# A decoder layer's set-up code: weight halves loaded first, projections side by side, two down-weight loads moved up

## The reference, cut to what matters

```python
def reference(x, ctx, Wi, Wf, Wg, w_norm, Wo, w, u, w_gate_up, w_down):
    # 1: i, f, g = x @ Wi.T, x @ Wf.T, x @ Wg.T; a = sigmoid(f)
    #    h = linear_scan(a, silu(i) * (1 - a)); xg = h * silu(g)
    #    y = xg * rsqrt(mean(xg**2) + eps) * w_norm;  x = layernorm(x + y @ Wo.T)
    # 2: x = layernorm(x + wkv(w, u, k=x, v=ctx))     # running sums of exp(k)*v and exp(k)
    # 3: gate, up = quant(x) @ quant(w_gate_up).T;  h = silu(gate) * up
    #    x = layernorm(x + quant(h) @ quant(w_down).T)
    return x
```

## Time and profile before

| | us |
|---|---|
| median of 3 runs | 411.18 (409.6 to 411.26) |
| profiled execution | 412.55 |
| its span | 410.1 |
| TensorE busy | 370.8 (90%) |
| VectorE busy | 353.6 (86%) |
| ScalarE busy | 318.7 (78%) |
| GpSimd busy | 219.3 (53%) |

### The profile page before, as it was taken

One profiled execution on the slowest core, in us unless ns is written; L12 is line 12 of the kernel. 1 busy time (PEld: TensorE's weight loads), 2 busy tenths in 40 slices (PEclk: granted clock), 3 DMA queues, 4 the chain that ended last, 5 costly groups with the idle time before them and its releaser, 6 DMA issues.

```text
span 410.1 us, 7960 instructions
## 1 busy us (share of the span) xinstructions
PE 370.8 (90%) x2774; PEld 289.9 (71%) x2774; DVE 353.6 (86%) x639; ACT 318.7 (78%) x420; POOL 219.3 (53%) x281
## 2 busy tenths in 40 slices
PE   7699899889997899999999999999999999659992
PEld 7698799768964788669775977497749785335541
DVE  3879898888788988988899988998899889898895
ACT  3677599769848989599959996799769994974782
POOL 1546772753355725674377535673566356644561
PEclk9989999999999999999999999999999999959999
DMA  7977456011110013000500050004000300000002
GB/s 257 361 273 269 164 195 243 2 53 27 59 46 0 2 48 134 0 28 2 179 2 27 2 179 2 26 0 154 25 0 26 129 0 0 26 2 18 36 26 77
DMA packets 12842, 31.74 MB, mean 77 GB/s; under 512 B 2038, under 2 KB 5132, under 8 KB 12812
## 3 DMA queue, kind: packets, MB, share of 16 engines
q1 hardware_dynamic: 12812, 31.35, 21.9%
HBM read 27.14 MB, written 4.21 MB: 76 GB/s over the span
## 4 chain that ended last, share of the span: by engine, by line
ACT 25%; PE 24%; issue 15%; DVE 14%; POOL 10%; POOLq 0%; ACTq 0%; DVEq 0%
PE proj_ps L530 13%; PE slot_ps L639 8%; POOL ring L1352 4%; ACT L1056 3%; ACT hqT L1021 2%; ACT ring L1014 2%; ACT L1060 2%; DVE inp L1545 2%; DVE x_max L1670 2%; ACT gate L897 2%; POOL gate L1292 2%; ACT q_state L962 2%; ACT q_state L956 2%; ACT gate L935 1%; ACT xqT L998 1%
## 5 line engine op out<-in xcount | busy, mean ns | idle before, releaser
L639 PE MATMUL slot_ps<-w1q,xqT 128*128 128x512 bf16 (+1 forms) x384 | 83.1, 367 | 5.1 <-DVE ring L1702 2.9
L1352 POOL TENSOR_TENSOR ring<-ring 128x512 f32<-128x512 f32 (+1 forms) x48 | 59.6, 1248 | 42.3 <-ACT ring L1007 41.1
L639 PEld LDWEIGHTS slot_ps<-w1q,xqT 128*128 128x128 bf16 x384 | 36.0, 99 | 44.7 <-issue 4.4
L530 PE MATMUL proj_ps<-x_high,proj_high 128*128 128x256 f32 x384 | 65.3, 292 | 1.7 <-DVE inp L1567 1.0
L530 PE MATMUL proj_ps<-x_high,proj_low 128*128 128x256 f32 x384 | 62.2, 284 | 0.0
L530 PE MATMUL proj_ps<-x_low,proj_high 128*128 128x256 f32 x384 | 62.0, 283 | 0.0
L530 PEld LDWEIGHTS proj_ps<-x_high,proj_high 128*128 128x128 f32 x384 | 53.6, 190 | 3.8 <-issue 1.6
L530 PEld LDWEIGHTS proj_ps<-x_high,proj_low 128*128 128x128 f32 x384 | 53.5, 191 | 0.0
L530 PEld LDWEIGHTS proj_ps<-x_low,proj_high 128*128 128x128 f32 x384 | 53.0, 189 | 0.0
L1327 POOL TENSOR_TENSOR den<-den,q_state 128x512 f32<-128x512 f32 x16 | 21.2, 1328 | 49.3 <-ACT q_state L962 48.9
L1007 ACT ACTIVATE ring<-ring,zero_bias,x_scale 128x512 f32<-128x512 f32 (+1 forms) x48 | 37.0, 775 | 9.5 <-DVE ring L1699 9.4
(11 more groups left out here) (157 smaller groups left out, 835.5 us busy)
## 6 DMA issues: line engine op xcount, KB each, us to landing
ring<-w_gate_up_dram SPq DMA_DIRECT2D x11, 512.0 KB, 4.2
forget<-xT_dram SPq DMA_DIRECT2D x8, 512.0 KB, 3.4
x_sb<-x_dram SPq DMA_DIRECT2D x8, 512.0 KB, 3.8
c_sb<-cT_dram SPq DMA_DIRECT2D x8, 512.0 KB, 4.5
out_dram<-late SPq DMA_DIRECT2D x12, 256.0 KB, 2.1
late<-w_down_dram SPq DMA_DIRECT2D x2, 704.0 KB, 6.9
ring<-w_down_dram SPq DMA_DIRECT2D x2, 704.0 KB, 4.2
scale_rows<-scratch_dram SPq DMA_DIRECT2D x2, 704.0 KB, 6.0
```

The costliest lines, as they stand in the source:

```text
L530: last = nc.tensor.matmul(out, a, b, start=(i == 0), stop=(i == len(terms) - 1))
L639: last = nc.tensor.matmul(slot_ps[:, s, half * 512:half * 512 + width], xqT[:, par, d, t * P:(t + 1) * P], w1q[:, d, half * I + at:half * ...
L1352: nc.gpsimd.tensor_tensor(hid, hid, gate_buf[:, at:at + width], ALU.mult).then_inc(hid_ready, 1)
```

## The change

It changes the order of the start-up part on all five queues, and nothing in the iteration or in the tail.

- SyncE: half (0,1) comes ahead of load 0, both i halves ahead of the column vectors and load 1; both output halves follow the g halves. Loads 8 and 9 are now the first two down rows (table `LOAD_AT`, from the place q in the queue to the load meant), and the pairs 8, 9, 10 follow as loads 10, 11, 12. Loads 13 and 14 remain down rows. The context `load_c(0)`, `store_scales` and `load_xT(2)` change places.
- TensorE: projections (0,0) and (0,1), (0,2) and (0,3), (1,0) and (1,1), (1,2) and (1,3) stand next to each other. Of the fillers, 28 in front of the first output projection, 16 in front of projection (1,0) and 36 in front of output projection (1,0) are gone. The key turning of batch 0 follows projection (1,1).
- VectorE, ScalarE, GpSimd: `weigh_rows`, `keep_rows` and `round_rows` move to match; `mean_square(0)` stands behind load 6 instead of 7; `layer_norm_2(0)` and the rest of the second norm move; the chunks' `scale_products`, `silu` and `hidden` of batch 0 are interleaved with WKV of batch 1 differently.

```diff
@@ -50,9 +50,10 @@
 RING = 3
 ROWS = 2 * IB + DB
-HOMES = [q % RING for q in range(UP_LOADS)] + [RING, RING + 1, 2, 1]
-
-SPREADS = [(0, IB, 6), (IB, 2 * IB, UP_LOADS), (2 * IB, ROWS, LOADS)]
+LOAD_AT = [0, 1, 2, 3, 4, 5, 6, 7, UP_LOADS, UP_LOADS + 1, 8, 9, 10, UP_LOADS + 2, UP_LOADS + 3]
+HOMES = [0, 1, 2, 0, 1, 2, 0, 1, RING, RING + 1, 2, 0, 1, 2, 1]
+
+SPREADS = [(0, IB, 6), (IB, 2 * IB, LOADS - 2), (2 * IB, ROWS, LOADS)]
 PROJ = 6
 U_CAP, U_FREE = 72.0, 16.0
...
@@ -462,39 +466,39 @@
             load_half((0, 0))
             load_xT(0)
+            load_half((0, 1))
             load_rows(0)
-            load_half((0, 1))
+            load_half((1, 0))
+            load_half((1, 1))
             load_columns()
-            load_half((1, 0))
             load_rows(1)
-            load_half((1, 1))
+            load_half((2, 0))
             load_rows(2)
-            load_half((2, 0))
             load_half((2, 1))
+            load_half((OUT_PROJ, 0))
+            load_half((OUT_PROJ, 1))
             load_rows(3)
             load_x(0)
             load_rows(4)
-            load_half((OUT_PROJ, 0))
             load_rows(5)
-            load_half((OUT_PROJ, 1))
-            load_rows(11)
+            load_rows(8)
             load_xT(1)
             load_rows(6)
             load_rows(7)
-            store_scales(0)
-            load_rows(8)
-            load_c(0)
-            load_rows(12)
             load_rows(9)
             load_rows(10)
-            load_rows(13)
+            load_c(0)
+            load_rows(11)
+            store_scales(0)
+            load_rows(12)
             spread_scales(0)
             load_x(1)
+            load_xT(2)
+            load_rows(13)
             store_scales(1)
             load_rows(14)
             load_c(1)
             spread_scales(1)
-            load_xT(2)
             load_x(2)
             store_scales(2)
             spread_scales(2)
...
@@ -687,13 +691,13 @@
                 pe.wait_ge(rows_rounded, q + 1)
                 wait(pe, rows_kept, q - 1)
-                if q == UP_LOADS:
-                    pe.wait_ge(scales_read, 2)
+                if LOAD_AT[q] >= UP_LOADS and row_slot(q) == 1:
+                    pe.wait_ge(scales_read, 1 if q < LOADS - 2 else 2)
                 if q == LOADS - 1:
                     pe.wait_ge(rows_kept, q)
                     pe.wait_ge(mlp_read, 2)
                 r = row_home(q)
-                if q < UP_LOADS:
+                if LOAD_AT[q] < UP_LOADS:
                     o = slot_16(row_slot(q), 2 * D).rearrange("p (d a o) -> p d a o", d=DB, a=2)
                     for a in range(2):
                         for d in range(DB):
...
@@ -710,6 +714,8 @@
             def turn_scales(k):
                 first, end, loads = SPREADS[k]
                 pe.wait_ge(row_scale_ready, loads)
+                if k == 1:
+                    pe.wait_ge(rows_kept, LOAD_AT.index(UP_LOADS + 1) + 1)
                 nc.tensor.transpose(scales_ps(k), row_scale[:, first:end],
                                     identity[:, :]).then_inc(scales_turned, 1)
...
@@ -760,61 +766,58 @@
             warm_up()
             warm_up()
             project(0, 0)
+            project(0, 1)
             turn_rows(0)
-            project(0, 1)
+            project(0, 2)
+            project(0, 3)
             turn_rows(1)
-            project(0, 2)
+            project(0, 4)
             turn_rows(2)
-            project(0, 3)
-            project(0, 4)
             project(0, 5)
-            for q in range(3, 6):
-                turn_rows(q)
-            turn_scales(0)
-            keep_busy(28)
-            pe.wait_ge(xg_ready, 1)
+            turn_rows(3)
             keep_busy(28)
             project_out(0, 0)
             sum_squares(0)
             project_out(0, 1)
-            turn_rows(6)
-            turn_rows(7)
-            keep_busy(16)
+            turn_rows(4)
+            turn_rows(5)
             project(1, 0)
-            turn_rows(8)
+            project(1, 1)
+            turn_scales(0)
             turn_keys(0, 0)
             turn_keys(0, 1)
-            project(1, 1)
-            turn_scales(1)
+            turn_rows(6)
             project(1, 2)
-            turn_rows(9)
             project(1, 3)
-            turn_rows(10)
+            turn_rows(7)
             project(1, 4)
             project(1, 5)
             keep_busy(28)
             turn_values(0, 0)
             turn_values(0, 1)
-            turn_rows(11)
-            keep_busy(36)
+            turn_rows(8)
+            turn_rows(9)
             project_out(1, 0)
             sum_squares(1)
+            turn_rows(10)
+            turn_rows(11)
+            turn_scales(1)
+            project_out(1, 1)
             turn_rows(12)
-            project_out(1, 1)
+            turn_inputs(0)
             project(2, 0)
-            turn_inputs(0)
-            turn_rows(13)
-            mlp_up(0, 0, 0, [0])
             turn_keys(1, 0)
             turn_keys(1, 1)
+            mlp_up(0, 0, 0, [0])
+            turn_rows(13)
+            project(2, 1)
+            project(2, 2)
             mlp_up(0, 0, 0, [1])
-            project(2, 1)
+            project(2, 3)
             mlp_up(0, 0, 0, [2])
-            project(2, 2)
-            turn_rows(14)
-            project(2, 3)
             project(2, 4)
             project(2, 5)
+            turn_rows(14)
             pe.wait_ge(mlp_read, 3)
             keep_busy(32)
             turn_values(1, 0)
...
@@ -1112,43 +1116,37 @@
             split_x(0)
             split_half((0, 1))
             split_half((1, 0))
+            read_projection(0, 0)
             split_half((1, 1))
-            read_projection(0, 0)
+            read_projection(0, 1)
             split_half((2, 0))
-            read_projection(0, 1)
             keep_rows(0)
             forget_gate(0)
+            read_projection(0, 2)
             split_half((2, 1))
+            split_half((OUT_PROJ, 0))
+            read_projection(0, 3)
             keep_rows(1)
-            read_projection(0, 2)
-            read_projection(0, 3)
-            split_half((OUT_PROJ, 0))
-            keep_rows(2)
             split_half((OUT_PROJ, 1))
             read_projection(0, 4)
+            keep_rows(2)
             read_projection(0, 5)
-            keep_rows(3)
-            read_scales(0)
             split_states(0)
             square(0)
             split_x(1)
+            keep_rows(3)
             keep_rows(4)
-            exp_tables()
-            decay()
-            for q in range(5, 7):
-                keep_rows(q)
-            silu_tables()
             normalise_1(0)
             read_projection(1, 0)
             exp_tables()
+            decay()
             exponential(0, 0)
             exponential(0, 1)
-            keep_rows(7)
             silu_tables()
             read_projection(1, 1)
-            keep_rows(8)
-            read_scales(1)
             read_projection(1, 2)
+            keep_rows(5)
+            read_scales(0)
             forget_gate(1)
             read_projection(1, 3)
             exp_tables()
...
@@ -1852,39 +1856,38 @@
             split_half((0, 0))
             split_first_x()
+            split_half((0, 1))
             weigh_rows(0)
-            split_half((0, 1))
-            weigh_rows(1)
             split_half((1, 0))
             split_half((1, 1))
+            weigh_rows(1)
+            biases()
             weigh_rows(2)
             split_half((2, 0))
+            split_half((2, 1))
+            weigh_inputs(0)
+            recurrence(0)
             weigh_rows(3)
-            split_half((2, 1))
-            weigh_rows(4)
-            weigh_inputs(0)
-            weigh_rows(5)
-            recurrence(0)
             split_half((OUT_PROJ, 0))
             gating(0)
             split_half((OUT_PROJ, 1))
             split_states(0)
-            biases()
-            for q in range(6, 8):
-                weigh_rows(q)
+            weigh_rows(4)
+            weigh_rows(5)
+            weigh_rows(6)
             mean_square(0)
             residual_1(0, 0)
             residual_1(0, 1)
             layer_norm_1(0)
+            weigh_rows(7)
             weigh_rows(8)
             weigh_rows(9)
-            weigh_rows(10)
-            weigh_rows(11)
             sum_weights(0, 0)
             denominator(0, 0)
             sum_weights(0, 1)
             denominator(0, 1)
             place_decay(0)
+            weigh_rows(10)
             sum_values(0, 0)
             sum_values(0, 1)
             numerator(0, 0)
...
@@ -1895,34 +1898,35 @@
             divide(0, 1)
             refine(0, 0)
             refine(0, 1)
+            weigh_rows(11)
             gating(1)
-            weigh_rows(12)
-            split_states(1)
             residual_2(0, 0)
             residual_2(0, 1)
+            split_states(1)
             layer_norm_2(0)
-            weigh_rows(13)
+            weigh_rows(12)
```

(21 more changed lines are left out.)

86 lines of the change are left out of this document (48 added, 38 removed).

## The result

The changed kernel took 406.62 us (median of 9 runs, 405.96 to 407.98) against 410.67 us of the kernel before (9 runs); the ratio is 0.9898 with a 95% interval of 0.9865 to 0.9932, so the change saves 4.1 us or 1.0%. The prediction was 408.5 us. The profiled span fell from 410.1 to 404.9 us.

The account below looks back on a forecast made before the run. No single engine but a relay bounds the start-up; TensorE is fullest in the loop. Leads of 2.0 and 3.4 us at the loop's first and third chunks, middle 2.7, give 411.18 - 2.7 = 408.5 us; range 405.6 to 411.8.

Parts of the forecast that it names:

- part 2: Ahead of the first output projection: TensorE idles 3.3 us, the clock falls; start at 36.4, 2.0 ahead, 1.5 given back.
- Part 1: First loads: half (0,1), third in the queue, lands at 9.0; low states end at 35.2 instead of 38.68, 3.5 us ahead.
- part 3: First norm of batch 0: second residual waits for the output projection alone; norm at 46.5, 3.8 us ahead.
- Parts 3 and 4: From batch 0's first norm to batch 1's: VectorE gives leads back, 0.7 us at batch 1's gating, 2.0 at its norm.
- Part 5: Interleaved chunks up to the loop: TensorE without idle time; loop's first chunk 2.0 us ahead, third 3.4; middle taken, 2.7.
- Half the gain: Start-up relay has more steps than charged, or half (0,1) lands no earlier; 1.2 us is left, 410.0; chance 0.17.
- A load in the place of the wait: Ahead of batch 1's weight scan: VectorE waits for late load 14, costing 2.5 us, time 411.0; chance 0.12.
- Slower by the clock: Without fillers both output projections of batch 1 run at clock 0.50, 5.8 us more, time 414.3; chance 0.08.
- More than forecast: No clock fall in the start-up and the loop keeps the 3.4 us lead: 406.2; chance 0.08.

Follow-up runs that it names:

- loads_old: Changed kernel with SyncE's first twelve loads back in the old order; 408.38 us, ratio 0.9939.
- weigh_late: Changed kernel with VectorE's weighing of load 11 behind the gating of batch 1 instead of ahead of it; 407.32 us, ratio 0.9894.
- late_only_busy: late_only with 44 filler transposes added ahead of batch 1's turned keys; 408.61 us, ratio 0.9944.
- late_only: Kernel before with only the late part of the start-up, behind the first norm of batch 1, in the new order; 411.39 us, ratio 1.0006.
- swap_only: Kernel before with GpSimd's last hidden product moved ahead of the first norm's root of batch 2; 409.63 us, ratio 0.9958.
- end_only: Kernel before with only the last steps ahead of the loop in the new order on all four engines; 408.21 us, ratio 0.9893.
- fillers: Changed kernel with filler transposes put back, in greater number, in TensorE's three idle stretches; 408.22 us, ratio 0.9900.

## Why the prediction was right, and where its sizes were off

**The direction and the places** held. Of the clock times of the laid-out order: low states 35.2 as their end (34.9 measured), first norm of batch 0 at 46.5 (46.35), first weight scan 52.9 (52.13), division 66.6 (66.16), gating of batch 1 70.7 (70.05), output projection (1,0) 73.7 (73.28), end of the pairing 77.4 (76.99), first norm of batch 1 87.2 (86.73). Of these none is off by a whole us (the output projection in part 2 is), and nearly all came a little earlier than forecast.

**Part 1** held in its sum and in its cause: the half lands at about 8.9, and the place in the queue counts (loads_old). The projection after it started at 9.31 + 2.88, 0.7 later than forecast, since x itself landed 0.8 later in this profile; in exchange the idle time ahead of load 0's turning was 1.12 and not 1.9, and the clock did not fall there.

**Part 2** forecast the wait (3.3; 2.90 measured), the fall, and the output projection's start at 36.4 (35.33). The 1.5 us that it gave back were a mis-sized term: with the clock held at 1.00, the way from the low states to the division of batch 0 is 0.26 shorter, and no more. The step that failed stands in part 3: the second residual waits "for the output projection alone". In the trace VectorE's residuals (41.94) stand behind its own weighing of loads 4 to 6, its mean square (40.91) and GpSimd's root (until 41.86). From the start to the first norm it takes 12.76 us with the fall and 12.69 in weigh_late without it. That the norm came at 46.35, with 46.5 forecast, is therefore partly luck: the output projection started 1.07 us earlier than forecast, and the way from it to the norm took 11.0 us instead of 10.1.

**Parts 3 and 4**: the leads given back on VectorE are there, 1.86 us for load 7 among them. The lead at the gating of batch 1 was thought to be 0.7; in the profile it is 1.35. At the norm of batch 1 it was thought to be 2.0, and is 2.44.

**Part 5 is where the size failed.** It said that TensorE carries a lead of 2.0 us through to the first chunk with nothing in the sum changing, and it took the middle of 2.0 and 3.4 for the time. Three things were mis-sized. The lead was not carried: 0.97 us of it is lost up to the gating of batch 2. That is the price of the new middle, which takes 24.86 us on the old early part too (late_only_busy), where the old middle takes 23.90. The last steps were charged with nothing up to the first chunk, and they bring 1.36 us: TensorE's waits of 1.31 and 0.99 us at 124.23 and 127.03 stood in the trace of before and were not read. And from the first to the third chunk it is 1.55 us (1.4 forecast), which stays in full, since the loop shows no relay that would take it back: each batch starts 4.4 us earlier. The forecast for the third chunk was 3.4 ahead; 4.4 was measured. Had it taken 3.4 and not the middle value, the prediction would have been 407.8. Of the 1.7 us between the forecast 2.7 and the 4.4, taking the middle value is 0.7, the lead at the norm 0.44, the waits less the lost lead 0.39, and the last piece 0.15.

**The rivals.** Half the gain did not occur. A load in the place of the wait: load 14 landed 4.1 us after its issue, as the row of before said, but VectorE wanted it 1.19 us before that and the wait was hidden, because the weight scan behind it waited another 1.33 us for ScalarE; the spread of scales was not waited for. Slower by the clock: both output projections did run with falls of the clock, each of three to four us, and holding the clock brought the time no lower; late_only shows that the mechanism is real one place further on, where it cost 3 us. The Trainium skill (TensorE: Matmul & The Clock Gate, Part 1), by which activity is what releases the throttle, points the right way about removed fillers, and the trace agrees (0.50 at 34 and at 75), though not every time: loads_old and weigh_late, with the same fillers removed, kept 1.00 at 34. It says nothing on whether the end waits for TensorE then. More than forecast, 406.2, is next to what came, though by another way: the fall happened, and did not matter.

## What to carry to other kernels

Before costing a reordering, list every idle time of the engine that is nearly full, up to the point where the steady part begins, and ask of each whether the new order keeps it; two waits of 2.3 us together were not read here, and they brought 1.36. A lead gained far ahead is worth what is left of it when the fullest engine takes over, and that has to be measured by distances between fixed places, not by start times, when the first transfers move the whole trace by a microsecond or more. Look for falls of the clock in every profile first: a distance with another fall in it says nothing about the edit. Two halves of a reordering tested alone can each show nothing: look in the trace whether the cut itself has opened an idle time.

## What was not expected of the hardware

The same idle time of TensorE is not always followed by a fall of the clock. swap_only and end_only have the same code up to here, and TensorE waits 1.81 and 1.80 us for load 7; then the clock is 1.00 in one and 0.50 in the other. The rows are TensorE's, and the stretch 48 to 49, first of swap_only, then of end_only:

```profile
46.13 0.62 PE L700 MATMUL slot_ps<-identity,ring 128*128 128x128 f16 x8 [1.81 <-POOL ring L1285]
46.59 1.06 PE L726 MATMUL slot_ps<-identity 128*128 128x128 f16 x16
...
48.00:49.00 1.00, 1.00 (x11) 1.00 (x10) 0.96 (x2) 0.00 (x0) 0.86 (x4) 1.00 0.61 147
```

```profile
46.23 0.62 PE L700 MATMUL slot_ps<-identity,ring 128*128 128x128 f16 x8 [1.80 <-POOL ring L1285]
46.69 1.79 PE L726 MATMUL slot_ps<-identity 128*128 128x128 f16 x16
...
48.00:49.00 1.00, 1.00 (x8) 1.00 (x6) 0.96 (x1) 0.00 (x0) 0.94 (x3) 0.50 0.69 168
```

Here, around the first norm of batch 0, the fall is on the path: 53.26 instead of 51.72 us to the norm of batch 1, in end_only and late_only alike, 1.54 us. It happened in two of the five profiles with the old early code. The new early code shows the same. TensorE waited 1.90 to 1.92 us at 42.8 to 44.7 in weigh_late, fillers and loads_old, and the clock fell in weigh_late alone (33.80 instead of 32.31 us to the division, 1.49). It waited 2.83 to 3.14 us for load 3 in eight profiles, and the clock did not fall near 34 in two of them, weigh_late and loads_old. A fall of the clock cost nothing that stands clear of the scatter (0.26 at most), 0.6, 1.5 or 3.0 us in this kernel, depending on who waited for TensorE behind it.

The start of one and the same code lay between 35.35 and 38.85 us in five profiles of the old early part, and between 32.68 and 33.59 in five of the new.
